# Group-norm steps and a slice's second moments moved from VectorE to ScalarE and TensorE in a one-core attention and selective-scan kernel

## The reference

```
# layer 0: block attention
xg   = group_norm(x)
xavg = mean of xg over 4 x 4 blocks          # 256 blocks of an image
A    = softmax((xavg Wq' + bq)(xavg Wk' + bk)' / sqrt(512))
out  = A @ (sums over 16 positions in a row of xg Wv' + bv)    # each repeated 16 times
x    = x + out
# layer 1: selective scan over the 4096 positions, 4 chunks of 128 channels, 256 inner channels, 16 states
h[s] = exp(dt * A[s]) * h[s] + dt * xc * B[s];   y = sum over s of h[s] * C[s]
x    = x + proj(layer_norm(chunks + mamba(layer_norm(group_norm(x)))))
```

## Time and profile before

| | |
|---|---|
| median of 3 runs (lowest to highest) | 16080.29 us (16077.08 to 16094.26) |
| profiled execution | 16090.54 us |
| its span, first to last instruction | 16088.7 us |
| VectorE busy | 14823.6 us, 92% |
| GpSimd busy | 14788.2 us, 92% |
| TensorE busy | 14186.2 us, 88% |
| ScalarE busy | 11509.9 us, 72% |
| mean granted TensorE clock | 0.947 |
| DMA read and written | 2376.15 MB and 150.99 MB, mean 158 GB/s |

### The profile page before, as it was taken

One profiled execution on the slowest core, in us unless ns is written; L12 is line 12 of the kernel. 1 busy time (PEld: TensorE's weight loads), 2 busy tenths in 40 slices (PEclk: granted clock), 3 DMA queues, 4 the chain that ended last, 5 costly groups with the idle time before them and its releaser, 6 DMA issues. The chain is left out here.

```text
span 16088.7 us, 151421 instructions
## 1 busy us (share of the span) xinstructions
PE 14186.2 (88%) x30720; PEld 5741.6 (36%) x30720; DVE 14823.6 (92%) x13024; ACT 11509.9 (72%) x18891; POOL 14788.2 (92%) x6275
## 2 busy tenths in 40 slices
PE   6988989889898898888889888899888898888888
PEld 2333333333333333333333333333333333333333
DVE  6999999999999999999999999999999999999998
ACT  5777767777677767777677776777767777677776
POOL 5999989999899989999899998999989999899998
PEclk8999999999999999999999999999999999999999
DMA  3444444444444444444444444444444444444444
GB/s 131 156 163 163 159 153 162 162 164 153 157 157 160 163 155 158 159 160 169 150 156 162 157 169 149 158 163 161 163 148 161 164 160 166 150 153 164 156 154 139
DMA packets 739082, 2537.63 MB, mean 158 GB/s; under 512 B 77241, under 2 KB 78017, under 8 KB 721729
## 3 DMA queue, kind: packets, MB, share of 16 engines
q1 hardware_dynamic: 738112, 2527.45, 46.1%
HBM read 2376.15 MB, written 150.99 MB: 157 GB/s over the span
## 5 line engine op out<-in xcount | busy, mean ns | idle before, releaser
L1460 POOL TENSOR_TENSOR RING<-RING,CS 128x1024 f32<-128x1024 f32 x4096 | 9597.9, 2363 | 1036.2 <-DVE RING L1150 973.3
L1150 DVE TENSOR_TENSOR_SCAN RING<-DA,HS,RING 128x512 f32<-128x512 f32 x8192 | 9946.1, 1265 | 496.9 <-ACT DA L777 451.1
L388 PE MATMUL YP<-RING,EYE 128*128 128x512 f32 x16384 | 8172.0, 632 | 1400.6 <-POOL RING L1460 1307.3
L777 ACT ACTIVATE DA<-ITEM,AN 128x512 f32<-128x512 f32 x8192 | 5495.8, 684 | 3017.5 <-DVE RING L1150 3001.5
L388 PEld LDWEIGHTS YP<-RING,EYE 128*128 128x128 f32 x16384 | 3126.8, 198 | 5995.0 <-issue 3596.3
L1130 DVE TENSOR_TENSOR RING<-DTP,BS 128x1024 f32<-128x1024 f32 x3072 | 3687.7, 1205 | 129.0 <-ACT DTP L847 117.6
L1447 POOL TENSOR_TENSOR RING<-ITEM,BS 128x1024 f32<-128x1024 f32 x1024 | 2421.3, 2365 | 10.0 <-DMA BS<-bc_rows 0.3
L388 PE MATMUL FL<-XN,WC 128*128 128x512 f32 x4096 | 1913.9, 611 | 9.8 <-ACT XN L866 4.6
L388 PEld LDWEIGHTS FL<-XN,WC 128*128 128x128 f32 x4096 | 821.4, 201 | 1087.4 <-issue 1079.1
L791 ACT ACTIVATE ITEM<-FL,COL 128x512 f32<-128x512 f32 x512 | 348.9, 682 | 1056.8 <-PE FL L388 1056.6
L388 PE MATMUL FL<-LS,WP 128*128 128x512 f32 x2048 | 983.2, 603 | 6.1 <-POOL LS L1482 6.1
(11 more groups left out here) (125 smaller groups left out, 10879.3 us busy)
## 6 DMA issues: line engine op xcount, KB each, us to landing
BS<-bc_rows SPq DMA_DIRECT2D x2048, 512.0 KB, 4.9
CS<-bc_rows SPq DMA_DIRECT2D x2048, 512.0 KB, 3.6
XR<-in_x SPq DMA_DIRECT2D x128, 1024.0 KB, 7.6
x_slices<-XR SPq DMA_DIRECT2D x64, 1024.0 KB, 8.3
XR<-x_slices SPq DMA_DIRECT2D x64, 1024.0 KB, 7.6
out<-XR SPq DMA_DIRECT2D x64, 1024.0 KB, 8.1
XR<-in_wqkv SPq DMA_DIRECT2D x24, 1024.0 KB, 7.8
bc_rows<-ROWS SPq DMA_DIRECT2D x256, 64.0 KB, 4.5
```

The source lines that it names most:

```text
L388: return pe.matmul(*a, **k)
L777: act.activation(DA[:, h, :], DT[:, i % 2, h, :], ACT.Exp, scale=AN[:, h, s:s + 1]).then_inc(dA_ready, 1)
L1150: dve.tensor_tensor_scan(H[:, slot(n), h, :], DA[:, h, :], U[:, slot(n), h, :], HS[:, i % ITEMS, h, s:s + 1], ALU.mult, ALU.add).then_inc( ...
L1460: pool.tensor_tensor(G[:, slot(n)], H[:, slot(n)], CS[:, s % C_ROWS, :].unsqueeze(1).broadcast_to([P, NH, T]), ALU.mult).then_inc(g_ready, 1)
```

## The change

The four bn_stats of a slice go. `slice_rows` now comes after s = 5 (j = 3) or s = 4 (j = 1) and `slice_blocks` after s = 9. ScalarE then makes the mean of each chunk from the block sums XS and the sum of squared deviations by Square over the whole slice, both with `accum_out`; it writes count, mean and squares into ST, from which bn_aggr works. VectorE sets the counts once. The next load into XT waits for `slice_squared`. The group norms' small steps move to ScalarE; the addition of squared deviation and variance becomes a second matmul into the same PSUM; `first_shift`, `second_shift` and the negated maximum are ScalarE's. TensorE's first `group_var` moves from s = 12 to s = 13.

```diff
@@ SyncE @@
-                sp.wait_ge(stats_done, b * NT + t)
+                sp.wait_ge(slice_squared, b * NT + t)          # load_stat; load_wq and the loads of the first slices likewise
@@ TensorE @@
-                            if s == 12:
+                            if s == 13:
                                 group_var(coming, 1)
...
-                mm(FP[:, 0:NCH], GM[:, :], GVAR[:, :], start=True, stop=True).then_inc(gvar_ready, 1)
+                mm(FP[:, 0:NCH], GM[:, :], GSQ[:, :], start=True, stop=False)
+                mm(FP[:, 0:NCH], GM[:, :], MV[:, :, 1] if n == 1 else V1[:, :], start=False, stop=True).then_inc(gvar_ready, 1)
@@ ScalarE, window @@
+                    if stat is not None:
+                        b, t = stat
+                        if s == 12:
+                            slice_means(t, b * NT + t + 1)
+                        if s == 13:
+                            slice_squares(XT, t, b * NT + t + 1, (0, 1))
+                        if s == 14:
+                            slice_squares(XT, t, b * NT + t + 1, (2, 3))
...
                         if j == 2 and not new:
+                            if s == 11:
+                                deviation(coming, 1)
                             if s == 14:
                                 group_rstd(coming, 1)
-                        if j == 2 and new and s == 1:
-                            group_rstd(coming, 2)
+                                first_shift(coming)
+                        if j == 2 and new:
+                            if s == 0:
+                                deviation(coming, 2)
+                            if s == 1:
+                                group_rstd(coming, 2)
+                                second_shift(coming)
@@ ScalarE, new functions @@
+            def slice_means(t, done):
+                act.wait_ge(stats_done, done)
+                for k in range(NCH):
+                    last = act.activation(S4[:, k, 0:SLICE_COLS], XS[:, k, t, :], ACT.Copy, scale=1.0 / T, accum_out=ST[:, k, t, 1:2])
+                last.then_inc(slice_mean, 1)
+            def slice_squares(src, t, done, ks):
+                if 0 in ks:
+                    act.wait_ge(slice_mean, done)
+                for k in ks:
+                    last = act.activation(src[:, k, :], src[:, k, :], ACT.Square, bias=ST[:, k, t, 1:2], scale=-1.0,
+                                          accum_out=ST[:, k, t, 2:3])
+                if NCH - 1 in ks:
+                    last.then_inc(slice_squared, 1)
+            def deviation(a, n):
+                act.wait_ge(gmean_ready, a * 2 + n)
+                act.activation(GMN[:, :], FP[:, 0:NCH], ACT.Copy, scale=-1.0).then_inc(gmean_kept, 1)
+                for k in range(NCH):
+                    mean = MV[:, k, 0:1] if n == 1 else M1[:, k:k + 1]
+                    last = act.activation(GSQ[:, k:k + 1], FP[:, k:k + 1], ACT.Square, bias=mean, scale=-1.0)
+                last.then_inc(dev_ready, 1)
+            # first_shift: 6 small activations, second_shift: 4; prob: 1 more (the negated maximum)
@@ VectorE, window @@
-                        if s == 3:
+                        if s == (5 if j == 3 else 4):
                             dve.wait_ge(x_stat, (b * NT + t) * 16 - (NT * 16 - 16))
-                            slice_moments(t, XT)
-                        if s == (9 if j == 3 else 12):
                             slice_rows(XT)
-                        if s == (12 if j == 3 else 14):
+                        if s == 9:
                             slice_blocks(t, b * NT + t + 1)
@@ VectorE, aggregate (deviation, first_shift, second_shift go) @@
-                dve.memset(GMS[:, :], 0.0)
...
-                dve.tensor_copy(GMS[:, :], MV[:, :, 0]).then_inc(x_aggr, 1)
@@ VectorE, first image's slices @@
-                slice_moments(t, src)
                 if t > 0:
-                    dve.wait_ge(stats_done, t)
+                    dve.wait_ge(slice_mean, t)
```

More of the change, by code:

```diff
@@ L122, in block_ssm_kernel @@
         OV = SM[:, 8:16].rearrange("p (k n) -> p k n", k=NCH)
-        DEV, GVAR, GLN, GRS, GSH, GRS16, GSH16 = (SM[:, 16 + 4 * n:20 + 4 * n] for n in range(7))
+        GLN, GRS, GSH, GRS16, GSH16 = (SM[:, 24 + 4 * n:28 + 4 * n] for n in range(5))
         MX, NMX, RSUM, RINV = (SM[:, 48 + 2 * n:50 + 2 * n] for n in range(4))
@@ L1039, in attention @@
             def attention():
+                deviation(0, 1)
                 group_rstd(0, 1)
+                first_shift(0)
                 pooled(0)
@@ L1053, in attention @@
                 attended(0, 1)
+                deviation(0, 2)
                 group_rstd(0, 2)
+                second_shift(0)
             def first_front(tile):
@@ L1081, in last_end @@
                 rstd(RS[:, :], var2_ready, log2_ready, rstd2_ready, tile + 1)
+            for t in range(NT):
+                slice_means(t, t + 1)
+                slice_squares((XF, XE, XT)[t % 3], t, t + 1, range(NCH))
             act.wait_ge(w_loaded, 16 * W_LOADS)
@@ L1096, in _ @@
             with act.Fori(0, BATCH - 1) as b:
-                for t in range(NT - 2):
+                for t in range(4):
                     for w in range(2, 2 + ITEMS):
-                        window(b * NT + t, w)
+                        window(b * NT + t, w, stat=(b + 1, t) if w == 3 else None)
+                for t in range(4, 6):
+                    for w in range(2, 2 + ITEMS):
+                        window(b * NT + t, w, stat=(b + 1, t + t - 4) if w == 3 else (b + 1, t + t - 3) if w == 5 else None)
                 for w in range(2, 4):
@@ L1208, in window @@
                     n = w * NS + s
+                    if coming is not None and j == 2 and not new and s == 5:
+                        dve.wait_ge(slice_squared, coming * NT + NT)
                     make_ahead(tile, n, d, first=first)
@@ L1238, in window @@
                                 aggregate(coming)
[L1239 to L1242, removed]
                         if j == 0:
@@ L1254, in window @@
                                 covariance(coming)
-                        if j == 2 and new:
-                            if s == 0:
-                                deviation(coming, 2)
-                            if s == 2:
-                                second_shift(coming)
             def link(a, n):
@@ L1264, in aggregate @@
             def aggregate(a):
[L1265 to L1266 removed]
                 for k in range(NCH):
                     last = dve.bn_aggr(MV[:, k, :], ST[:, k].rearrange("p t n -> p (t n)"))
[L1269 to L1271 removed]
+                last.then_inc(x_aggr, 1)
                 dve.wait_ge(x_aggr, a + 1)
[L1274 to L1297 removed]
             def score_max(a):
@@ L1348, in attention @@
                 dve.memset(XN[:, :, 0:HALO], 0.0).then_inc(halo_kept, 1)
+                dve.wait_ge(counts_set, 1)
+                dve.wait_ge(slice_squared, NT)
                 aggregate(0)
-                deviation(0, 1)
-                first_shift(0)
                 score_max(0)
@@ L1356, in attention @@
                 covariance(0)
-                deviation(0, 2)
-                second_shift(0)
                 dve.wait_ge(gshift_ready, 2)
```

82 lines of the change are left out of this document (35 added, 47 removed).

## The result

The changed kernel takes 16,021.6 us (median of 6 runs, 16,015.5 to 16,023.8) against 16,090.6 us (6 runs) of the kernel before: ratio 0.9957, 95% interval 0.9946 to 0.9968. The spans of the two profiled executions are 16,021.9 and 16,088.7 us. The sign and the range of the forecast (15,996) held, and its gain of 84 us came to 69 in the medians; several of its terms did not hold.

A forecast was written before the change was run, and what follows sets the result against it. VectorE and GpSimd, both 92% busy, bound it by place; a tile lasts 231 us plus GpSimd's waits. Per image 19.7 gained, 9.0 lost; times 7 is 75, with the first image 84: 15,996 us; 8-in-10 range 15,928 to 16,072.

The forecast's parts named there:

- rival C: ScalarE's slice work delays copy L847 and exponentials of steps 13 to 15; up to +207 us, 16,203; chance 0.09.
- D: Rival: small steps no faster on ScalarE, so terms 7 and 3.3 don't come; +72 us, 16,068; chance 0.07.
- One sign of being wrong: The prediction is wrong if a first slice (w = 3, tiles 0 to 5) costs more than 3 us.
- First slices: w = 3, tiles 0 to 5, 42 windows: slice_blocks after step 9 costs 1.5 us each, between 0 and 3.7.
- rival B: Longer waits in steps 5 to 10 lower TensorE's clock in the next convolution; 42 x 1.3 = 55 us, 16,051; chance 0.16.
- rival A: Early reductions in first slices cost nothing, as tiles with and without a slice take 242.4; 63 us more saved, 15,933; chance 0.18.
- The sign that these tiles stay at 242.4: The last image's eight tiles stay at 242.4 us; if they move, the reasoning by places is wrong.
- Second slices: w = 5, tiles 4 and 5, 14 windows: GpSimd's waits before G4 and G9 shrink; gain 1.8 us, bounds 0 and 4.0.
- Windows after them: Windows following the second slices: VectorE gains a lead; saves 1.2 us in tile 5 and 4.6 in tile 6 (bounds 1.4, 5.7).
- what the small steps gain: Tile 6: deviation and first_shift leave VectorE for ScalarE; gain 7 us, bounds 3.6 and 7.3.
- Tile 7: TensorE's wait of 3.63 us for VectorE's deviation goes, plus 0.3 for second_shift; gain 3.3 us, bounds 2 and 6.
- The first image: Eight slices ahead of the loop end 12 us sooner, 3 given back by ScalarE; gain 9 us, bounds 5 and 12.

The follow-up runs named there:

- E3: Kernel before with one line changed: in the first slices slice_blocks stands after step 9 instead of 12; 16,159.8 us against 16,083.1.
- E4: Changed kernel with one line changed: in the first slices slice_blocks stands after step 11 instead of 9; some 65 us faster, of 140 expected.
- E7: Changed kernel plus one 0.94 us matmul in TensorE's wait in every window j = 2; 15,994 to 16,007 us, ratio 0.9954 to the kernel before.
- E2: Kernel before with only the slices' second moments on ScalarE and the reductions at their new places; 16,131.8 us against 16,083.1.
- E1: Kernel before with only the group norms' small steps moved to ScalarE and TensorE, slices keeping bn_stats and places; ratio 0.9933 to the kernel before.
- E12: E5 plus zero-weight matmuls only where TensorE's wait holds them: one in windows j = 2, two in windows j = 0 at step 14; 15,826.4 us.
- E9: E5 plus zero-weight matmuls: one in windows j = 2, six in each window's steps 12 to 14; slower than the kernel before.
- E5: Changed kernel with, in the first slices, slice_blocks after step 11 instead of 9 and slice_rows after step 4 instead of 5; 15,891.9 us.
- E11: Changed kernel plus a tensor_tensor and a tensor_scalar on 4 columns on VectorE in windows w = 4 outside the attention's tiles; 16,155.1 us against 16,021.6.

## Why the prediction was right, and where it was not

Much of the approach by places held. Tile 6 was forecast at 255.4 and came to 254.9, and G5 to G10 at 19.4 and came to 19.5. VectorE's wait for the copy DTP at the end of w = 3 went from 1.1 to 2.0 us, far from the several of rival C. ScalarE's wait for TensorE in tile 7 (before L987, now L1019) went from 6.1 to 2.5 us, which speaks against D.

The sum per image was 10.7 and came to 9.2, but in part by luck, as errors of both signs cancelled. Tiles 0 to 3 lost 12.6 us together instead of 6.0. Tiles 4 and 5 gained 3.6 instead of 1.8, tile 6 11.7 instead of 11.6 and tile 7 6.5 instead of 3.3. One sign of being wrong that the prediction had set was met in part: a first slice was not to cost more than 3 us, and it cost 4.2 in tile 0 and 3.1 in the mean of tiles 0 to 3. The terms:

- **First slices**, 1.5 each, measured 2.6 to 2.9 in tiles 1 to 3 and 4.2 in tile 0. The 1.5 of VectorE's order is there to 0.2 (E3, E4). Most of the rest is rival B's mechanism at another place: I looked for it in the convolution of w = 3, and it came in the mean of LV in w = 2, 28 times of 35. E3, E4 and E7 show it. In tile 0 the clock takes more. Its w = 2 lasts 62.6 us in the first image and 64.1 to 66.7 in the six others. In the second image (66.5) the LV mean is slow, and TensorE already enters the window in part at 1.2 GHz (granted clock 0.65 against 1.00 before), after a wait of 3.43 us, so that the convolution is slow too. TensorE there, after and before:

```profile
2286.57 2.95 PE L388 MATMUL YP<-RING,EYE 128*128 128x512 f32 x4 [3.43 <-issue]
2289.31 4.37 PE L388 MATMUL FL<-XN,WC 128*128 128x512 f32 x8
```

```profile
2297.34 1.98 PE L388 MATMUL YP<-RING,EYE 128*128 128x512 f32 x4 [2.83 <-POOL RING L1460]
2299.15 3.60 PE L388 MATMUL FL<-XN,WC 128*128 128x512 f32 x8
```

- **The equal 242.4 us** of tiles with and without a slice, on which rival A rested. In the kernel before, w = 3 of the last image's tile 4 is 1.9 us shorter than that of tile 3 of the earlier trace rows (61.38 against 63.24), but its w = 2 is 1.5 longer (61.86 against 60.36), as its LV mean is slow. That holds for four of the last image's tiles 0 to 6, and tile 2, where it is not slow, takes 240.8. So no slack absorbed the 2 us of a slice: where the slice is missing, the clock takes most of them back. The sign that these tiles stay at 242.4 was badly chosen: they were 240.8 to 242.4 before and are 240.7 to 243.2 after, with a mean of 242.0 in both.
- **Second slices**, 1.8 each, measured w = 5 of tiles 4 and 5 shorter by 3.6 and 4.3, around the upper bound of 4.0: both waits of the earlier trace rows went, where I had kept 2.2 us.
- **Windows after them**, 1.2 and 4.6. Of the 1.2, window w = 2 of tile 5 shows 0.4 (62.0 to 61.6). The 4.6 of tile 6 is not the slices' (E2). I had put to the slices what the small steps gain, 10.7 (E1) against 7 forecast with a bound of 7.3 (7.2 by its rows), so the sum of tile 6 came out right for a wrong split. Which part of E1's 10.7 is the copy and memset in `aggregate` was not tried alone.
- **Tile 7**, 3.3, measured 6.5, above its bounds. Its upper bound of 6 left out that the clock can give back. The first fence is TensorE after; the earlier trace rows are its counterpart, and the second fence is the convolution behind them before:

```profile
4015.92 6.40 PE L388 MATMUL YP<-RING,EYE 128*128 128x512 f32 x8
4022.16 0.51 PE L388 MATMUL FL<-SM,GM 128*128 128x4 f32 x4
4023.20 3.70 PE L388 MATMUL FL<-XN,WC 128*128 128x512 f32 x8 [0.54 <-ACT SM L1019]
```

```profile
4039.51 5.81 PE L388 MATMUL FL<-XN,WC 128*128 128x512 f32 x8 [0.54 <-ACT SM L987]
```

From the start of the sums to the second small matmul it was 9.7 us (4028.66 to 4038.39) and is 6.2: the wait of 3.63 has gone. The convolution behind it takes 2.1 less, at a granted clock of 1.00 instead of 0.63. The Trainium skill, TensorE: Matmul & The Clock Gate, "What's actually happening", has the throttled state as the default that activity lifts. This place and E7 agree: with the wait gone or filled, the matmuls behind it ran at 1.00. Which waits are harmless these runs do not show (see the end).
- **The first image**, 9, measured 2 to 4 (kernels with the same start have their first G from 182.6 to 185.1). E2 alone gives 6.9; E1 alone costs 4.4, a term that I left out. GpSimd has no products there, so VectorE's small operations take 0.16. The same steps last 4.4 us on ScalarE (TensorE's first small matmul to `pooled`, 55.17 to 59.55) against 3.2 before. In E1 each of the two group norms costs 1.1 in this way, and the other half is TensorE's clock: after them the LV mean of the first tile takes 6.69 instead of 5.50 us and the LS mean 6.32 instead of 5.40. VectorE's reductions end 9.4 us sooner, then it waits for ScalarE's last squares and table load:

```profile
50.74 1.28 ACT L1150 ACT_TABLE_LOAD   x1
...
52.29 0.18 DVE L1424 TENSOR_SCALAR AN<-AN 128x32 f32<-128x32 f32 x1 [3.46 <-ACT AN L1151]
```

Together the errors left 17 us of 84. It stays open why the lower level falls on just these places. E3 changes only when VectorE does a reduction, and TensorE's rows in w = 2 are alike up to the slow matmuls, the wait ahead of them included (0.76 us before, 0.72 in E3, both in tile 3).

## What to carry to other kernels

Split a change into its halves before keeping it: here one half was worth 0.67% and the other cost 0.30%. Put extra work where the engine waits, not where it sets the pace: the same two reductions cost 3.8 us after steps 5 and 9 and nothing in w = 3 inside the waits ahead of steps 4 and 5 (61.1 to 61.4 against 61.4 without a slice), though w = 2 gives some of it back. Where TensorE resumes after a wait on the critical path, a harmless matmul that fits wholly inside the wait can pay (E12, 0.5%; E7 alone was not clear); too many delay the sums and cost more (E9, 2.3% over E5).

## What was not expected of the hardware

- TensorE's clock can take back in one window what another engine saved in the window before. After a wait of 0.76 us the next four matmuls ran partly at 1.2 GHz in 28 of 35 tiles. Yet the wait does not decide it alone: the same rows with the same wait met 1.00 in 32 of 35 tiles before, and in w = 4 of tile 4 the same wait of 2.62 us was followed by 1.98 us in one kernel and by 3.50 in another. With the wait of 0.76 filled none of the 35 was slow (E7, E9, E12), whether by a real matmul or by ones with a column of zeros as weights.
- A VectorE tensor_tensor on 4 columns takes 1.89 us beside GpSimd's products in E11 and 0.16 in the first image, ahead of them; a tensor_scalar with one input takes 1.21. The Trainium skill, SBUF — State Buffer, "Who interferes with whom", says that a VectorE operation with two inputs in SBUF contends with one of GpSimd that reads SBUF, and that tensor_scalar can in some forms. E11 agrees, and adds the price: on 4 columns, the rest of the 2.35 us product that is running.
